# Query, key and value projections of batches 1 to 7: from full fp32 products to three fp32r products of rounded parts and rests

## The reference

```python
q = einsum('bld,ed->ble', x, Wq) + bq     # and k, v alike; d = e = 256
scores = einsum('bhqd,bhkd->bhqk', q, k) * scale + bias_causal
attn = softmax(scores)
out = einsum('bhqk,bhkd->bhqd', attn, v)
return einsum('bld,ed->ble', out, Wo) + bo
```

## Time and profile before

| | |
|---|---|
| median of three runs | 4040.36 us |
| the three runs | 4034.44, 4040.36, 4056.86 us |
| the profiled execution | 4003.07 us |
| its span, first to last instruction | 4001.3 us |
| mean granted clock of TensorE | 0.991 |
| busy: PE, DVE, ACT, POOL | 3896.2, 2953.2, 2764.6, 932.6 us |

### The profile page before, as it was taken

How to read it: one execution, slowest core, us unless ns; L and a number is a source line. 1 busy time by engine, 2 the same in 40 slices (tenths; PEclk the granted TensorE clock), 3 DMA queues, 4 the chain that set the end, 5 groups by cost and what they waited for, 6 DMA issues and landing times.

```text
span 4001.3 us, 107790 instructions
## 1 busy us (share of the span) xinstructions
PE 3896.2 (97%) x42129; PEld 2406.8 (60%) x42129; DVE 2953.2 (74%) x3826; ACT 2764.6 (69%) x5702; POOL 932.6 (23%) x1610
## 2 busy tenths in 40 slices
PE   7999999999999999999999999999999999999998
PEld 4555555555555555556875555555555555557854
DVE  7788888888888888884048887888888778882074
ACT  2677777777777777775257777777777777774265
POOL 3101111111111234332023332333333232120021
PEclk8899999999999999999999999999999999999999
DMA  5332233323233333335643334333333323335622
GB/s 161 69 73 62 63 91 87 79 78 92 76 86 83 88 103 106 86 104 176 215 137 102 94 90 100 91 101 102 95 103 95 91 76 98 71 87 194 204 69 80
DMA packets 276106, 405.75 MB, mean 101 GB/s; under 512 B 64522, under 2 KB 190930, under 8 KB 262738
## 3 DMA queue, kind: packets, MB, share of 16 engines
q1 hardware_dynamic: 272526, 390.47, 36.6%
q0 software_dynamic: 3072, 8.39, 0.8%
HBM read 264.30 MB, written 121.73 MB: 96 GB/s over the span
## 4 chain that ended last, share of the span: by engine, by line
PE 89%; DVE 4%; ACT 3%; issue 2%; DMA 1%; SPq 1%; POOL 1%; ACTq 0%; DVEq 0%; POOLq 0%
PE ps_acc L1161 25%; PE ps_r L1100 19%; PE ps_p L1130 16%; PE ps_r L1197 6%; PE ps_p L1265 5%; PE ps_r L1277 5%; PE ps_r L1201 3%; ACT probs L985 3%; PE ps_r L1205 3%; PE ps_r L1105 2%; DVE part_max L1472 2%; PE ps_p L1124 2%; PE ps_p L1137 1%; PE ps_r L1190 1%; PE ps_r L1096 1%
## 5 line engine op out<-in xcount | busy, mean ns | idle before, releaser
L1472 DVE TENSOR_REDUCE part_max<-ps_p 128x2 f32<-128x1024 f32 (+3 forms) x2560 | 2622.2, 1061 | 606.9 <-PE ps_p L1130 437.2
L985 ACT ACTIVATE probs<-ps_r 128x512 f32<-128x512 f32 (+1 forms) x4608 | 2332.0, 575 | 660.1 <-PE ps_r L1100 406.8
L1100 PE MATMUL ps_r<-q_stack,k_stack 54*128 54x512 f32 (+3 forms) x5120 | 1375.8, 392 | 31.2 <-ACT probs L985 28.1
L1130 PE MATMUL ps_p<-k_stack,q_stack 52*128 52x512 f32 (+3 forms) x5120 | 1239.5, 425 | 26.5 <-DVE part_max L1472 16.9
L1161 PE MATMUL ps_acc<-probs,v_head 128*17 128x256 f32 x19456 | 1145.1, 361 | 1.8 <-ACT probs L985 1.6
L1100 PEld LDWEIGHTS ps_r<-q_stack,k_stack 54*128 54x128 f32 x5120 | 725.9, 187 | 263.0 <-ACT probs L985 218.1
L1161 PEld LDWEIGHTS ps_acc<-probs,v_head 128*17 128x17 f32 x19456 | 489.2, 97 | 465.8 <-issue 222.2
L1130 PEld LDWEIGHTS ps_p<-k_stack,q_stack 52*128 52x128 f32 x5120 | 559.5, 186 | 322.4 <-issue 165.2
L1105 PE MATMUL ps_r<-id,mk 64*128 64x64 bf16 x3598 | 284.4, 194 | 0.0
L1577 DVE COPY xf<-ps_r 128x256 f32<-128x256 f32 x52 | 22.1, 425 | 350.0 <-PE ps_r L1277 350.0
L938 POOL TENSOR_TENSOR bk<-bk,y_sb 128x256 f32<-128x256 f32 x104 | 76.2, 732 | 874.4 <-ACT y_sb L1032 874.3
(11 more groups left out here) (160 smaller groups left out, 2346.6 us busy)
## 6 DMA issues: line engine op xcount, KB each, us to landing
probs<-w_dram SPq DMA_DIRECT2D x58, 1024.0 KB, 5.8
q_stack<-parts SPq DMA_DIRECT2D x378, 128.0 KB
k_stack<-parts SPq DMA_DIRECT2D x378, 128.0 KB
parts<-pa SPq DMA_DIRECT2D x128, 256.0 KB, 2.6
parts<-pb SPq DMA_DIRECT2D x128, 256.0 KB, 3.4
o_sums<-acc_sb SPq DMA_DIRECT2D x1008, 17.0 KB
swp<-tmp SPq DMA_DIRECT2D x128, 128.0 KB, 2.6
bk<-recips SPq DMA_DIRECT2D x58, 256.0 KB
```

The source lines that it names most:

```text
L985: act.activation(probs[:, at % PBUF, u, 0:w], block_bank(g, n, u)[:, 0:w], ACT.Exp)\
L1100: mm = pe.matmul(bank[:, col:col + QW - q0], ks[s][r, kb * P:(kb + 1) * P], qs[s][r, qt * QW + q0:(qt + 1) * QW], start=fresh, stop=True, ...
L1130: mm[u] = pe.matmul(banks[:, u, col:col + w], qs[s][r, qb * P:(qb + 1) * P], ks[s][r, kc * QW:kc * QW + w], start=fresh, stop=True, skip_g ...
L1472: mm = dve.tensor_reduce(part_max[:, :, qb, kc], ps_p[:, p1_banks(g, n), col:col + w], AX_X, ALU.max)
```

## The change

For batches 1 to 7 the turned rows and the weights are each split into a part rounded to fp32r and a rest, also fp32r. Each matmul of a `qk` or `v` job becomes three fp32r matmuls into the same bank: rounded rows times rounded weights, rests of the rows times rounded weights, and rounded rows times the rests of the weights. Batch 0 keeps its fp32 products (from `w_first`).

What goes with it:

- `xT` holds one half chunk (256 rows) instead of a whole one. A new POOL job `xs` stands one step behind each `xt`: a cast and two subtractions make `x_high` and `x_low`. ACT's next `xt` copy waits for the split of the one before (`xs_split`), and so do the first `qk` jobs.
- The first weights are split by POOL after batch 0's ahead jobs (`w_split`). Those of attention B are loaded into idle memory in round 2 (`wl`), split in round 3 (`wp`, twice), stored to DRAM in round 4 (`ws`), and loaded from there as two transfers where one stood.
- For room, `PBUF` goes from 8 to 6, `y_sb` from four row tiles to two (so ACT's copy waits for the POOL addition of two jobs before instead of four), and the experts' first weight matrices lie partly in `cs` and `tmp`, each load written as two transfers. Some buffers of the last stage move too.

```diff
 SLOTS = 3
 RING = 3
-PBUF = 8
+PBUF = 6
...
             nxt = (f, c + 1) if c + 1 < NQ else (f + 1, 0)
             if nxt[0] < NB:
                 out += rows(nxt[0], nxt[1], x1 + 2)
-            out += [(x0, ("xt", f, c, 0)), (x1, ("xt", f, c, 1)), (x1 + 3, ("cs", f, c, 0))]
+            out += [(x0, ("xt", f, c, 0)), (x0 + 1, ("xs", f, c, 0))]
+            out += [(x1, ("xt", f, c, 1)), (x1 + 1, ("xs", f, c, 1)), (x1 + 3, ("cs", f, c, 0))]
             for kind, u in TURN[c]:
...
+NEXT_WEIGHTS = ((2 * STEPS + 30, "wl", 0), (3 * STEPS + 10, "wp", 0), (3 * STEPS + 22, "wp", 1), (4 * STEPS + 30, "ws", 0))
...
-        wqkv = sb("wqkv", [P, KD, 3 * D])
+        wqkv = sb("wqkv", [P, KD, 3 * D], F32R)
+        wqkv_low = sb("wqkv_low", [P, KD, 3 * D], F32R)
...
         xl = sb("xl", [P, CH, D])
-        xT = sb("xT", [P, KD, CW])
+        xT = sb("xT", [P, KD, D])
+        x_high = sb("x_high", [P, 2, KD, D], F32R)
+        x_low = sb("x_low", [P, 2, KD, D], F32R)
...
-        y_sb = sb("y_sb", [P, CH, D])
+        y_sb = sb("y_sb", [P, 2, D])
...
-        w1_sb = [probs_f[:, 4096 * s:4096 * s + KD * FF].rearrange("p (k f) -> p k f", k=KD) for s in range(2)]
-        w2_sb = [probs_f[:, 4096 * s + KD * FF:4096 * s + 4096].rearrange("p (f d) -> p f d", f=NF) for s in range(2)]
+        w1_sb = [probs_f[:, FF * k:FF * (k + 1)] for k in range(KD)], \
+            [x[:, :, :].rearrange("p k n -> p (k n)") for x in (cs, tmp)]
+        w2_sb = [probs_f[:, 2 * FF * (s + 1):2 * FF * (s + 2)].rearrange("p (f d) -> p f d", f=NF) for s in range(2)]
+        w1_first = [xb[:, 4 * k:4 * (k + 1), :].rearrange("p a d -> p (a d)") for k in range(KD)]
+        w_first = bk[:, :, :, :].rearrange("p a k n -> p (a k n)")[:, 0:WCOLS].rearrange("p (k n) -> p k n", k=KD)
...
+                elif kind == "wl":
+                    sp.wait_ge(job_mm, JOB_PLACE[BESIDE_JOBS[-1]] + 1)
+                    sp.dma_start(next_low.rearrange("p (k n) -> p k n", k=KD), w_b.rearrange("(k p) n -> p k n", p=P))\
+                        .then_inc(next_in, 16)
+                elif kind == "ws":
+                    sp.wait_ge(next_split, KD)
+                    for j, w in enumerate((next_high, next_low)):
+                        sp.dma_start(w_d[j], w).then_inc(next_stored, 16)
                 elif kind == "zl":
...
             def load_w1(to, e, done):
-                sp.dma_start(to, w1[bass.ds(e, 1), :, :].rearrange("o (k p) f -> p (o k) f", p=P)).then_inc(done, 16)
+                for k in range(KD):
+                    sp.dma_start(to[k], w1[bass.ds(e, 1), k * P:(k + 1) * P, :].rearrange("o p f -> p (o f)")).then_inc(done, 16)
...
             for g in range(NG):
                 if g % PAIRS == 0 and g // PAIRS == B - 1:
                     sp.wait_ge(job_mm, JOB_PLACE[("v", B - 1, NQ - 1, CH - 1)] + 1)
-                    sp.dma_start(wqkv[:, :, :], w_b.rearrange("(k p) n -> p k n", p=P)).then_inc(weights_in, 16)
+                    sp.wait_ge(next_stored, 32)
+                    for i, w in enumerate((wqkv, wqkv_low)):
+                        sp.dma_start(w[:, :, :].bitcast(F32), w_d[i].rearrange("p (k n) -> p k n", k=KD))\
+                            .then_inc(weights_in, 16)
                 if g % PAIRS == 0 and g // PAIRS == B + 1:
...
+            def split(high, low, x, step, nth, out_sem):
+
+                pool.tensor_copy(high, x).then_inc(step, 1)
+                pool.wait_ge(step, nth + 1)
+                for h in range(0, 3 * D, D):
+                    mm = pool.tensor_tensor(low[:, h:h + D], x[:, h:h + D], high[:, h:h + D].bitcast(F32), ALU.subtract)
+                mm.then_inc(out_sem, 1)
+
...
+                elif kind == "xs":
+                    nth = 2 * (NQ * (f - 1) + c) + i
+                    pool.wait_ge(ring_used, PLACE[("xt", f, c, i)] + 1)
+                    pool.tensor_copy(x_high[:, i, :, :], xT[:, :, :]).then_inc(xs_step, 1)
+                    pool.wait_ge(xs_step, nth + 1)
+                    for k in range(KD):
+                        pool.tensor_tensor(x_low[:, i, k, :], xT[:, k, :], x_high[:, i, k, :].bitcast(F32), ALU.subtract)\
+                            .then_inc(xs_split, 1)
+                elif kind == "wp":
+                    pool.wait_ge(next_in, 16)
+                    cols = slice(3 * D * i, 3 * D * (i + 1))
+                    split(next_high[:, cols].bitcast(F32R), next_low[:, cols].bitcast(F32R), next_low[:, cols], next_step, i, next_split)
...
             for j in AHEAD:
                 job(*j)
+            pool.wait_ge(weights_in, 16)
+            for k in range(KD):
+                split(wqkv[:, k, :], wqkv_low[:, k, :], w_first[:, k, :], w_step, k, w_split)
...
-                        pool.tensor_tensor(rows, rows, y_sb[:, i, :], ALU.add).then_inc(res_out, 1)
+                        pool.tensor_tensor(rows, rows, y_sb[:, i % 2, :], ALU.add).then_inc(res_out, 1)
                         return
-                    pool.tensor_tensor(rows, rows, y_sb[:, i, :], ALU.add).then_inc(res_step, 1)
+                    pool.tensor_tensor(rows, rows, y_sb[:, i % 2, :], ALU.add).then_inc(res_step, 1)
...
                 if kind == "xt":
-                    act.activation(x_turned(f, c)[:, :, 2 * i * P:2 * (i + 1) * P], ring(at)[:, :].rearrange("p (k n) -> p k n", k=KD),
+                    if f:
+                        nth = 2 * (NQ * (f - 1) + c) + i
+                        if nth:
+                            act.wait_ge(xs_split, KD * nth)
+                    act.activation(x_turned(f, c, i), ring(at)[:, :].rearrange("p (k n) -> p k n", k=KD),
                                    ACT.Copy).then_inc(ring_used, 1)
...
                     n = CH * (NQ * f + c) + i
-                    if n >= CH:
-                        act.wait_ge(res_out, n - CH + 1)
-                    act.activation(y_sb[:, i, :], ring(at)[:, 0:D], ACT.Copy).then_inc(ring_used, 1)
+                    if n >= 2:
+                        act.wait_ge(res_out, n - 1)
+                    act.activation(y_sb[:, i % 2, :], ring(at)[:, 0:D], ACT.Copy).then_inc(ring_used, 1)
...
                 elif kind == "qk" and i == 0:
-                    pe.wait_ge(ring_used, PLACE[("xt", f, c, 1)] + 1)
-                    pe.wait_ge(weights_in, 16 * (ly + 1))
+                    if f == 0:
+                        pe.wait_ge(ring_used, PLACE[("xt", f, c, 1)] + 1)
+                        pe.wait_ge(weights_in, 16)
+                    elif c == 0:
+                        pe.wait_ge(w_split, KD)
+                        pe.wait_ge(weights_in, 16 + 32 * ly)
                 elif kind == "y":
                     if i == 0:
                         pe.wait_ge(o_scaled, 2 * KD * (NQ * f + c + 1))
                     pe.wait_ge(wo_in, 16 * (ly + 1))
+                if f and kind == "qk" and i < 2:
+                    pe.wait_ge(xs_split, KD * (2 * (NQ * (f - 1) + c) + i + 1))
...
                     half, proj = divmod(u, 2)
-                    lo = proj * D + half * P
+                    w = slice(proj * D + half * P, proj * D + (half + 1) * P)
                     for k in range(KD):
-                        mm = pe.matmul(to[:, 0:D], wqkv[:, k, lo:lo + P], x_turned(f, c)[:, k, j * D:(j + 1) * D],
-                                       start=(k == 0), stop=(k == KD - 1))
+                        if f == 0:
+                            mm = pe.matmul(to[:, 0:D], w_first[:, k, w], x_turned(f, c, j)[:, k, :],
+                                           start=(k == 0), stop=(k == KD - 1))
+                            continue
+                        pe.matmul(to[:, 0:D], wqkv[:, k, w], x_high[:, j, k, :], start=(k == 0), stop=False)
+                        pe.matmul(to[:, 0:D], wqkv[:, k, w], x_low[:, j, k, :], start=False, stop=False)
+                        mm = pe.matmul(to[:, 0:D], wqkv_low[:, k, w], x_high[:, j, k, :], start=False, stop=(k == KD - 1))
                 elif kind == "v":
+                    w, j, rows = slice(2 * D, 3 * D), i // 2, slice(i % 2 * P, (i % 2 + 1) * P)
                     for k in range(KD):
-                        mm = pe.matmul(to[:, 0:D], x_turned(f, c)[:, k, i * P:(i + 1) * P], wqkv[:, k, 2 * D:3 * D],
-                                       start=(k == 0), stop=(k == KD - 1))
+                        if f == 0:
+                            mm = pe.matmul(to[:, 0:D], x_turned(f, c, j)[:, k, rows], w_first[:, k, w],
+                                           start=(k == 0), stop=(k == KD - 1))
+                            continue
+                        pe.matmul(to[:, 0:D], x_high[:, j, k, rows], wqkv[:, k, w], start=(k == 0), stop=False)
+                        pe.matmul(to[:, 0:D], x_high[:, j, k, rows], wqkv_low[:, k, w], start=False, stop=False)
+                        mm = pe.matmul(to[:, 0:D], x_low[:, j, k, rows], wqkv[:, k, w], start=False, stop=(k == KD - 1))
```

43 lines of the change are left out of this document (32 added, 11 removed).

## The result

The changed kernel took 4024.58 us (median; 4015.57 to 4034.47, one execution of 19 ms left out), the kernel before in the same session 4044.35 (4034.44 to 4056.86). The ratio is 0.9952, 95% interval 0.9936 to 0.9968: 20 us (13 to 26) where 57 were predicted. The time lies just above the predicted range.

A forecast was written before the change was run, and what follows sets the result against it. PE was taken to bound the kernel: 336 jobs at 0.192 us save 64.5 us, less 10% is 58, less one for the rest 57; carried in proportion from 4040.4 this gives 3983 us, range 3955 to 4020.

The forecast's parts named there:

- the bounds of 0.107 and 0.124: Start-to-start price in us of one new 256-column fp32r matmul on PE, taken as 0.112; savings of 74.6 and 40 us.
- rival 2: Weight loads not hidden under 107 ns matmuls on PE: distance 0.19 us, 93 us longer, 4134 us; chance 0.05.
- the rule of the Trainium skill: Weight loads overlap matmuls only across row groups: a job 1.28 us against 0.97, 105 us slower; left out of the sums.
- Six records of 0.112 are 0.67 us where four of 0.216 were 0.86: 0.192 us less: PE's saving in each projection job of batches 1 to 7; over 336 jobs 64.5 us.
- a `qk` job of 0.78 us: Sign to look for: PE time from a job's first start to the next matmul, instead of 1.06 us.
- So even there nearly all arrives: Tightest cycle, four full steps and a `qk` job, DVE waiting 0.27 us: a pass moved up 0.19 still follows its reduction.
- I let 10% go: Share of PE's 64.5 us saving taken not to reach the kernel's time, leaving 58 us.
- Rival 1: The saved time goes to ACT and DVE: only a fifth arrives, 13 us, 4027 us; chance 0.07.
- The mean wait of 0.53 us: ACT's average wait for PE before copies after `qk` and `v`, more than twice the 0.19 a job shrinks; held against rival 1.
- even the upper bound costs about nothing: Attention B's weights as two loads, 11.2 us plus 0.4 issue, would end at 1430.8, their reader having started at 1430.88.
- rival 3: A new wait on split, SyncE's queue or two-deep `y_sb`: 1 us in 56 `xt` copies; half gives 4012 us; chance 0.06.
- The sign of idle time: Sign of a wrong forecast: PE's idle time growing by more than about 25 us.

The follow-up runs named there:

- e3: Kernel before with three fp32r matmuls per projection matmul of batches 1 to 7, all on rounded rows and unsplit weights, without the splits and other extras: 4005.1 us, ratio 0.9899.
- e14: Kernel before with plain transfers for POOL's indirect ones and each VectorE maximum over half its columns: 3957.57 us, ratio 0.9773.
- e15: Kernel before with three fp32r products on rounded rows, no extras, plain transfers for indirect ones, and halved VectorE maxima: 3912.39 us, ratio 0.9659.
- e1: Kernel before, unchanged, run again for a second profile: ratio 1.000, profiled span 4055.9 us.
- e9: Changed kernel without the second of round 24's two weight transfers, the first layer's low part staying in place: 4017.31 us, ratio 0.9934.
- e2: Changed kernel, unchanged, run again for a second profile: ratio 0.9945, profiled span 4013.0 us.
- e8: Changed kernel with the low part of the second layer's weights loaded in round 24 after the load of `lr`: 4029.24 us, ratio 0.9948.
- e4: Changed kernel with all its splits, loads and buffers, but fp32 projection matmuls on the rounded parts, rests unused: 4052.39 us, ratio 1.0023.
- direct rows: POOL's 64 indirect transfers made plain ones of as many rows, routing left out: changed kernel 3970.15 us, kernel before 3992.97 us.
- e11: Kernel before with POOL's 64 indirect transfers replaced by plain ones of as many rows, routing left out: 3992.97 us, ratio 0.9868.

## Why the prediction was wrong, step by step

**Right.** What the new matmuls do to TensorE, and the sign of the change. Records 0.118 us apart, inside the bounds of 0.107 and 0.124. The exposed first load of a job stays. The weight loads are hidden, so rival 2 is out. Out with it is the rule of the Trainium skill (TensorE: Matmul & The Clock Gate, packing small matmuls) that loads overlap only across row groups: by the prediction's estimate from it 105 us more were due, and here the loads of six full-height matmuls in a row were hidden, but for the first. And the splits on POOL, `PBUF` 6, `y_sb` of two and the experts' loads cost nothing in the undisturbed stretch (377.32 against 377.47).

**Mis-sized: "Six records of 0.112 are 0.67 us where four of 0.216 were 0.86: 0.192 us less".** Measured 0.16 (0.90 against 1.06): 54 us in place of 64.5. 0.112 came from records of 128 columns streamed twice; a record of 256 streamed once takes 0.118, six times 0.006 is 0.036 us a job, which is the whole difference. The sign "a `qk` job of 0.78 us" was a slip beside it: it leaves out the 0.09 us from the last record to the next matmul, which the 1.06 holds, and by the prediction's own sum should have read 0.87.

**Failed: "So even there nearly all arrives" and "I let 10% go".** 35% went, to VectorE: 35 us of 54 arrive (e3's stretch), and 94% arrive once its maxima are halved (e14, e15). The step that failed is the reading of the tight cycle of the earlier trace rows: "moved up by 0.19 it would start at 666.04, just after". I had found the right reduction, the one that began at 664.77 and ended at 666.00, but held the *matmul* of the next pass against it, at 666.23. The pass first needs its weight load, and that load too waits for the reduction. It already stood right behind it before the change, and the matmul 0.18 us later:
```profile
666.04 0.19 PEld L1130 LDWEIGHTS ps_p<-k_stack,q_stack 52*128 52x128 f32 x2
```
So the slack was 0.05 us and not 0.23. The same cycle after the change, PE, its loads, then DVE:
```profile
656.41 0.39 PE L1275 MATMUL ps_r<-x_high,wqkv 128*128 128x256 f32 x1
```
```profile
657.87 0.19 PEld L1198 LDWEIGHTS ps_p<-k_stack,q_stack 52*128 52x128 f32 x2 [0.21 <-DVE part_max L1557]
```
```profile
656.59 4.82 DVE L1557 TENSOR_REDUCE part_max<-ps_p 128x2 f32<-128x1024 f32 x4 [0.91 <-PE ps_p L1198]
662.25 1.23 DVE L1557 TENSOR_REDUCE part_max<-ps_p 128x2 f32<-128x1024 f32 x1 [0.84 <-PE ps_p L1198]
```
The first reduction begins 0.18 us after the job and takes 1.23, as it did before. It ends at 657.82, the load starts 0.05 us behind it as before, and now TensorE stands for it. The pass, of which the trace has the matmul 0.03 us behind its load, begins earlier by the whole 0.155 us that the job gave, but the scores behind it come only 0.08 us earlier than before, counted from the start of the job (worked out). From 656.59 to 662.25 the cycle is 5.66 us, against 5.74 before:
```profile
664.77 1.23 DVE L1472 TENSOR_REDUCE part_max<-ps_p 128x2 f32<-128x1024 f32 x1 [0.91 <-PE ps_p L1130]
666.26 3.49 DVE L1472 TENSOR_REDUCE part_max<-ps_p 128x2 f32<-128x1024 f32 x3 [0.27 <-PE ps_p L1130]
670.51 1.23 DVE L1472 TENSOR_REDUCE part_max<-ps_p 128x2 f32<-128x1024 f32 x1 [0.76 <-PE ps_p L1130]
```
VectorE is not full in this cycle: it works 4.7 us of the 5.66 and waits for PE twice (the row of four holds a wait of 0.11 us behind the first, worked out). It is the length of one reduction, beside a job that got shorter, that holds the pass.

The jobs of rounds 5 to 11 lose their time at this place on average too. I laid the starts of the same PE records of e1 and e3 beside each other, from the start of each of 40 jobs (worked out): on average 0.155 us are saved 1.1 us after the start and 0.157 at 1.6 us, 0.117 at 1.9, 0.101 at 2.3, and 0.102 still at 5.0 us. In e14 and e15, with halved maxima, 0.155 and 0.156 at the first two are followed by 0.152 at 2.3 and at 5.0. In e15 the reduction of this cycle is done at 637.14, long before the load that needs it, at 637.52, which waits no more:
```profile
636.45 0.69 DVE L1487 TENSOR_REDUCE part_max<-ps_p 128x2 f32<-128x512 f32 x1 [1.44 <-PE ps_p L1137]
```
```profile
637.52 0.19 PEld L1137 LDWEIGHTS ps_p<-k_stack,q_stack 52*128 52x128 f32 x2
```
Rival 1 named VectorE with a chance of 0.07 and overstated it (a fifth arriving; 65% did). The mean wait of 0.53 us that I set against it was ScalarE's, at its copies, and says nothing of VectorE.

**Failed in one place: "even the upper bound costs about nothing".** The second weight load costs 5 us in round 24 (e9). I asked when PE needs the weights, and not what stands behind the load on SyncE's queue: the store of the maxima, the wait for it, then `lr`. That is rival 3, at one place where I had set its price by 56.

**The sign of idle time.** It was to be wrong if PE's idle time grew by more than about 25 us. It went from 105 to 144 us in the first two profiles, but from 131 (e1) to 145 (e2) in the second two. The sign came in one pair and not in the other, since single profiles differ by as much.

**The sum again.** 35 us that arrive, less 5 in round 24, leave 30. Measured: 20 (13 to 26) and 22 (14 to 31). Where the other 10 are, or whether they are noise, stays open. Round 1 is not the place, though it is longer with the change (56.2 us in after and e3, 54.6 in e1): TensorE was granted 0.50 of full speed there in after, e2 and e3 (the windows 168 to 173, 170 to 175 and 166 to 171 us) and 1.00 in before and in e8, which has the whole change and takes 54.3. Rounds 0 and 1 together take 110.7 and 110.5 us in the two profiles of before, 109.5 and 110.6 after.

One can leave out the rounds in which the indirect transfers and the experts run, 26 to 33 and 58 to 62 (all worked out). The rest of the span is 2913.6 and 2916.9 us in the two profiles of before, 2897.0 and 2888.1 in those of the changed kernel, 2885.2 in e3 and 2917.4 in e4: 17 to 29 us for the change, 28 to 32 for the products. The 13 rounds left out take 1087.6 and 1139.0 us in before, 1135.5 and 1124.9 after. There, and there alone, the first profile of the changed kernel was the longer one, by 48 us. Whether the extras lose something there stays open (round 32 alone takes 61.6 and 61.5 us in the changed kernel, 55.0 and 59.4 in before, 58.3 in e3, and 53.9 against 54.3 with direct rows). I had carried the saving over from the profiled 4003 to the median by proportion; that was harmless, but that profile, with few stops, was no fair picture of before.

## What to carry to other kernels

When an engine is made faster, look for the first instruction behind the faster place that needs something of another engine, and measure its slack where that instruction begins: for a matmul at its weight load, here 0.18 us ahead of the matmul. A mean wait of another instruction is not that slack (0.53 us here, against 0.05), nor is the idle time of the other engine in the cycle (1.0 us here). The share of the saving that arrived fell from 89% to 65% to 37% as PE's load shrank; an experiment that adds work to the bound engine and one that removes it show this bend at once.

An added transfer is costed by what the queue issues behind it, above all a store that the queue itself then waits for. And where single profiles differ by 1% without any change, take two of each kernel, and compare an undisturbed stretch of many rounds: it repeated to 0.3 us in 377 (377.28, 377.47 and 377.58 in before, e1 and e11).
